# State space stage of a five-block network: where its normalisation, SiLU and first and last group stand in the order

## The chip, the cores and the metric

One core of a Trainium2 chip runs the whole program. The metric is the time of one execution on the device, in microseconds, of which the state space stage is one part in six. The engines are TensorE (matrix products; PE in the rows), VectorE (DVE), ScalarE (ACT), GpSimd (POOL) and SyncE (SP), which issues the loads. Each runs its own instructions in the order in which they are written, and the engines wait for each other by semaphores.

## The reference

`x` has shape (4, 1024, 256). The program computes six sublayers in turn, each on a layer norm of `x`: a gated recurrent layer, attention, the recurrent layer again, a mixture of experts, the state space layer (the "S" stage), the mixture again. The change touches the state space layer alone:

```
xn = rmsnorm(layernorm(x), norm_w)               # both norms in one scale and shift per token
z, x_ssm, B, C, dt_raw = split(xn @ in_proj_w.T) # 512, 512, 128, 128, 8 columns
x_conv = silu(conv_b + sum_k conv_w[k] * x_ssm shifted by k)       # 4 taps
dt = softplus(dt_raw + dt_bias);  dA = exp(-exp(A_log) * dt)       # 8 heads
h_t = h_(t-1) * dA_t + (dt_t * x_t) B_t;   y_t = h_t . C_t + D * x_t     # h_0 = 0
x = x + layernorm(x) + (y * silu(z)) @ out_proj_w.T
```

## The kernel before

The scan over 1024 positions is computed in chunks of 128. A tile is one chunk of one sequence. A group `p` (0 to 7, `PT` = 8) holds the four tiles (`b` = 0 to 3, `GT` = 4) of the four sequences at the same chunk, and the state `H` of each sequence goes from group to group. `n` = 4p + b is the tile's number. `groups` runs a loop over pairs of groups 0 to 5, and groups 6 and 7 behind it; its last argument `left` says whether two, one or no groups follow.

For a tile, `y` is a product within the chunk and one with the state: `tile_y` (L1509 by the decay matrix `dec`, L1512 by `H` and `rise`, the decays from the chunk's start times C). `tile_state` (L1520) computes what the chunk adds to the state. `tile_out` (L1528) multiplies the gated `y` by the output weights. The other engines feed it. ScalarE makes `dec` from `lb`, the loaded sums of decays (`decays`: eight L1630 and one L1633, for the tile `AHEAD` = 2 further on), reads the projections out of PSUM (`unit`: units dt, B, C, four of x, four of z, 11 a group, in three banks in turn), applies SiLU to the convolution (L1664) and to z, normalises a later group into `xn` (L1647) and turns `X` into its residual with `restore` (L1656). `hi` (L1639) and VectorE's `low` (L1724) split the turned `xn` for the products at full precision. VectorE also computes statistics (L1709 to L1717), convolution steps (L1735), `weigh` (L1765), `times_dt` (L1771), `gate` (L1781, L1786), `update_state` (L1792) and the residual (L1800). GpSimd makes scales and shifts in `norms` (L1853 to L1858), the rise products `scale_c` (L1867), `scale_x` (L1875) and `decay_state` (L1881). SyncE loads `lb` and `rise` for each tile, 512 KB each.

While group p is computed, the projections and the convolution of group p + 1 are made in pieces, one behind each tile (`piece`), and the normalisation of group p + 2 at `b` = `SCALE_AT`, its scales at `b` = `NORM_AT`. The order is written out by hand in each engine's `group`. At the border of two groups, these lines meet: TensorE's unit z3 reuses the bank of z0 and so waits for ScalarE's read of it; `turn_x` waits for SiLU of the whole convolution; VectorE has in its order `weigh` of the next tile 0, the statistics of group p + 2 and only then `times_dt` of tile 0, behind which the second `turn_x` and the first `tile_y` wait.

## Time and profile before

| | us |
|---|---|
| median of 3 runs | 1934.23 (1933.54 to 1936.37) |
| the profiled execution, its own time | 1933.88 |
| its span | 1932.1 |
| state space stage, 1322.9 to 1706.0 | 383.10 |
| in it TensorE busy | 339.28 |
| ScalarE busy | 273.38 |
| VectorE busy | 269.69 |
| GpSimd busy | 186.34 |

The time of an execution is a little more than its span, which runs from the first instruction to the last. Busy time of TensorE's matrix products, which overlap, is modelled; an engine's share says nothing by itself of what the others wait for. In the timeline rows the idle time before an instruction and what ended it stand in square brackets.

### The profile page before, as it was taken

How to read it: one execution, taken by the hardware profiler on the slowest of the kernel's cores; microseconds unless marked ns; L12 is line 12 of the kernel's file. 1: busy time of each engine (PE TensorE's matmuls, PEld its weight loads, DVE VectorE, ACT ScalarE, POOL GpSimd, SP SyncE). 2: the span in 40 equal slices, each digit the busy share in tenths (PEclk: the TensorE clock that was granted, in tenths of full speed). 3: DMA queues.
4: the chain of work that ended last, by engine and by line, in shares of the span. 5: the costliest groups of instructions: out<-in, count | busy, mean ns of one | idle time of the engine just before them, and what ended most of it. 6: DMA issues, size and time to landing. Idle time of an engine off the chain costs nothing. (4 is left out here: it accounts for less than half of the span.)

```text
span 1932.1 us, 30828 instructions
## 1 busy us (share of the span) xinstructions
PE 1752.0 (91%) x9742; PEld 1156.5 (60%) x9742; DVE 1340.6 (69%) x2878; ACT 1130.9 (59%) x1624; POOL 901.4 (47%) x654
## 2 busy tenths in 40 slices
PE   5999787999999999997999799997898899989998
PEld 4888673222222222227888677776676676767776
DVE  4545895777777777775555588885677777768886
ACT  3323588999999999994333222213777777622220
POOL 0001116999999999994002232211554445521111
PEclk9999898999999999998999999998999999999999
DMA  4000165534535435300000000001322222300000
GB/s 152 1 0 11 65 186 103 83 44 62 69 43 72 58 46 83 45 1 12 1 0 21 23 17 0 0 0 33 125 89 88 88 88 88 121 2 22 22 21 23
DMA packets 57640, 96.96 MB, mean 50 GB/s; under 512 B 7936, under 2 KB 29664, under 8 KB 57568
## 3 DMA queue, kind: packets, MB, share of 16 engines
q1 hardware_dynamic: 55392, 94.50, 21.7%
q10 hardware_dynamic: 2176, 1.55, 0.2%
q8 instruction: 39, 0.64, 0.1%
q14 instruction: 33, 0.27, 0.0%
HBM read 78.98 MB, written 17.04 MB: 50 GB/s over the span
## 5 line engine op out<-in xcount | busy, mean ns | idle before, releaser
L1232 POOL TENSOR_TENSOR att_weights<-att_weights 128x1024 f32<-128x1024 f32 x288 | 541.0, 1893 | 17.7 <-DVE att_weights L1176 7.3
L1176 DVE SCALAR_TENSOR_TENSOR att_weights<-att_weights,ps 128x512 f32<-128x512 f32 x576 | 370.1, 684 | 152.3 <-ACT att_weights L1152 150.5
L1152 ACT ACTIVATE att_weights<-att_weights 128x1024 f32<-128x1024 f32 x288 | 302.5, 1051 | 0.0
L1148 ACT ACTIVATE att_weights<-ps 128x1024 f32<-128x1024 f32 x288 | 294.1, 1022 | 9.9 <-PE ps L1094 5.6
L720 DVE SCALAR_TENSOR_TENSOR X<-ps,moe_gsel,X 128x256 f32 (+1 forms) x512 | 246.6, 484 | 64.4 <-PE ps L47 48.4
L1108 PE MATMUL ps<-att_weights,att_v_ones 128*32 128x512 f32 (+3 forms) x1536 | 288.8, 497 | 2.6 <-POOL att_weights L1232 2.5
L47 PE MATMUL ps<-w_experts_hi,moe_xh 128*128 128x512 f32 x512 | 205.2, 401 | 0.0
L47 PE MATMUL ps<-w_experts_hi,moe_xl 128*128 128x512 f32 x512 | 203.1, 397 | 0.0
L47 PE MATMUL ps<-w_experts_lo,moe_xh 128*128 128x512 f32 x512 | 201.6, 394 | 0.0
L313 ACT ACTIVATE ffn_gates<-ps,ffn_gate_bias 128x512 f32<-128x512 f32 x96 | 66.1, 688 | 207.2 <-PE ps L47 200.8
L1091 PE MATMUL ps<-q_stack,k_stack 128*128 128x512 bf16 (+3 forms) x384 | 116.8, 341 | 29.5 <-DVE att_weights L1176 19.8
L780 POOL TENSOR_TENSOR X<-X,moe_bias_sb 128x512 f32 (+1 forms) x32 | 41.5, 1298 | 207.6 <-DVE X L720 206.4
L103 POOL TENSOR_TENSOR ffn_rstd<-ffn_var,ffn_power 128x4 f32<-128x4 f32 x16 | 16.2, 1011 | 259.4 <-DVE ffn_var L135 259.4
L1091 PE MATMUL ps<-att_q_stack,att_k_stack 128*128 128x512 bf16 (+3 forms) x384 | 114.3, 332 | 22.6 <-DVE att_weights L1176 17.6
L1091 PEld LDWEIGHTS ps<-q_stack,k_stack 128*128 128x128 bf16 x384 | 37.3, 98 | 154.9 <-DVE att_weights L1176 143.0
L1091 PEld LDWEIGHTS ps<-att_q_stack,att_k_stack 128*128 128x128 bf16 x384 | 37.0, 96 | 149.7 <-DVE att_weights L1176 142.7
L47 PEld LDWEIGHTS ps<-w_experts_hi,moe_xh 128*128 128x128 f32 x512 | 96.0, 188 | 26.8 <-DVE X L720 3.3
L1108 PEld LDWEIGHTS ps<-att_weights,att_v_ones 128*32 128x32 f32 x1536 | 56.9, 108 | 90.0 <-issue 54.1
L47 PEld LDWEIGHTS ps<-w_experts_lo,moe_xh 128*128 128x128 f32 x512 | 96.1, 188 | 22.3
L47 PEld LDWEIGHTS ps<-w_experts_hi,moe_xl 128*128 128x128 f32 x512 | 96.1, 188 | 20.5
L629 ACT ACTIVATE moe_gT<-ps 96x512 fp32r<-96x512 f32 x16 | 9.5, 593 | 160.0 <-PE ps L560 160.0
L1867 POOL TENSOR_TENSOR ssm_rise<-ssm_rise,ssm_cT 128x512 f32<-128x512 f32 x64 | 94.5, 1502 | 18.0 <-DMA ssm_rise<-decays 18.0
(257 smaller groups left out, 3881.4 us busy)
## 6 DMA issues: line engine op xcount, KB each, us to landing
ssm_lb<-decays SPq DMA_DIRECT2D x32, 512.0 KB, 4.5
ssm_rise<-decays SPq DMA_DIRECT2D x32, 512.0 KB, 3.8
qk_parts<-qkv_part SPq DMA_DIRECT2D x32, 384.0 KB, 2.6
q_stack<-qk_parts SPq DMA_DIRECT2D x64, 128.0 KB, 4.5
k_stack<-qk_parts SPq DMA_DIRECT2D x64, 128.0 KB, 8.2
att_q_stack<-qk_parts SPq DMA_DIRECT2D x64, 128.0 KB, 4.6
att_k_stack<-qk_parts SPq DMA_DIRECT2D x64, 128.0 KB, 8.0
out<-X SPq DMA_DIRECT2D x8, 512.0 KB, 2.9
```

The source lines that it names most:

```text
L47: ins = pe.matmul(out, l(k), r(k), start=first and n == 0, stop=last and n == len(passes) - 1)
L103: pool.tensor_tensor(self.rstd[:, s], self.var[:, s], self.power[:, :], ALU.pow).then_inc(self.rstd_done, 1)
L313: act.activation(gates[:, m, gate], ring[:, u % RING], ACT.Tanh if gate == 2 else ACT.Sigmoid, bias=gate_bias[:, gate * KC + m:gate * KC + ...
L720: dve.scalar_tensor_tensor(out=x, in0=ring[:, e // 2, (e % 2) * C:(e % 2 + 1) * C], scalar=gsel[:, s, j, e:e + 1], in1=x, op0=ALU.mult, op ...
L780: pool.tensor_tensor(x, x, bias_sb[:, pair], ALU.add).then_inc(added, 1)
L1091: ins = pe.matmul(scores(u)[:, t, c:c + w], SK[s][:, h, kj * P:(kj + 1) * P], SQ[s][:, h, q:q + w], start=True, stop=not diagonal)
L1108: ins = pe.matmul(O(qb)[h * 2 * HD:(h + 1) * 2 * HD, q0:q0 + w], va[:, s, kj, h], Wt[:, u % WU, t, c:c + w], start=kj == 0, stop=m in BLOC ...
L1148: act.activation(Wt[:, u % WU], scores(u), ACT.Exp).then_inc(exp_done, 1)
L1152: act.activation(Wt[:, u % WU], Wt[:, u % WU], ACT.Ln, bias=1.0).then_inc(ln_done, 1)
L1176: dve.scalar_tensor_tensor(out=wt[:, t], in0=wt[:, t], scalar=LIMIT, in1=scores(u)[:, t], op0=ALU.min, op1=ALU.max).then_inc(max_done, 1)
L1232: pool.tensor_tensor(Wt[:, u % WU], Wt[:, u % WU], Wt[:, u % WU], ALU.mult).then_inc(sq_pool, 1)
L1867: ins = pool.tensor_tensor(heads, heads, cT[:, v, b].unsqueeze(1).broadcast_to([P, NH // 2, P]), ALU.mult)
```

## The change

In steady groups, `SCALE_AT` goes from 2 to 0 and the normalisation (now `apply`, then `restore`) stands behind that tile's decays, and the edges stand ahead of the decays at `b` = 2. SiLU of the convolution is two activations, the first of which waits for two convolutions of the four. `turn_in` waits for one unit fewer. Group 0 is taken out of the loop, and with it group 5: the loop now runs over pairs from 1 to 4. Group 0 has no state before it, so the products by `H`, `rise` and its loads, `scale_c` and `decay_state` are left out, and the update is a copy. Group 7 makes no state. In the head, `hi(0)` waits for its own load of `norm_w`, `restore(0)` follows it, the second statistics stand ahead of what waits for `neg_a`, `restore(1)` and the first two decays go into group 0 behind SiLU.

```diff
-        NORM_AT, SCALE_AT = 0, 2
+        NORM_AT, SCALE_AT = 0, 0
...
+            group(0, 0, 2)
+            with eng.Fori(0, PT // 2 - 2) as i:
                 group(i * 2 + 1, 1, 2)
+                group(i * 2 + 2, 0, 2)
+            group(PT - 3, 1, 2)
             group(PT - 2, 0, 1)
             group(PT - 1, 1, 0)
...
             def turn_in(p):
-                pe.wait_ge(unit_read, 3 + p * UNITS)
+                pe.wait_ge(unit_read, 2 + p * UNITS)
...
-                    for r in range(2):
+                    for r in range(0 if starts(p) else 2):
                         ins = pe.matmul(ps_y[r * DH:(r + 1) * DH, cols], H[:, b, 2 * f + r], rise[:, b % 2, 2 * f + r],
...
-                    tile_state(p, v, b)
+                    if left:
+                        tile_state(p, v, b)
...
-                act.wait_ge(conv_step, (p + 1) * FT * (TAPS - 1))
-                act.activation(xc[:, v], xc[:, v], ACT.Silu).then_inc(xc_done, 1)
+                half = FT // 2
+                for f in (0, half):
+                    act.wait_ge(conv_step, (p * FT + f + half) * (TAPS - 1))
+                    ins = act.activation(xc[:, v, f:f + half], xc[:, v, f:f + half], ACT.Silu)
+                ins.then_inc(xc_done, 1)
...
+                if starts(p):
+                    decays(0, v, 0, p)
+                    decays(1, v, 1, p)
...
+                    if starts(p) and b == 0:
+                        restore(p + 1)
...
+                    if left and b == 2:
+                        edges(p + 1, 1 - v)
                     if left or b + AHEAD < GT:
                         decays(n + AHEAD, v if b + AHEAD < GT else 1 - v, (b + AHEAD) % GT, p + (b + AHEAD) // GT)
...
-                        normalise(p + 2)
+                        apply(p + 2)
+                        restore(p + 2)
...
-            act.wait_ge(norm.xn_done, 1)
+            act.wait_ge(norm_in, 16)
+            hi(0)
...
-            dve.memset(H[:, :, :, :], 0.0).then_inc(h_done, GT)
...
+            statistics(1)
+            piece(0, 0, 0)
...
-                decay_state(v, p * GT, 0)
+                decays = left and not starts(p)
+                if decays:
+                    decay_state(v, p * GT, 0)
...
+            sp.dma_start(norm_w[:, :], c_dram["norm_w"]).then_inc(norm_in, 16)
```

How this moves instructions shows on two engines. ScalarE, in the loop at b = 0, before: from the decays of tile 2 to the read of unit B (`dtT` is the read of unit dt, `bT` of B).

```order
L1630 ACTIVATE ssm_dec<-ssm_lb,ssm_l_tok 128x128 x8
L1632 REGISTER_ALU
L1633 ACTIVATE ssm_dec<-ssm_dec 128x1024
L1567 ISA
L1582 ACTIVATE ssm_dtT<-ps,ssm_dt_bias 8x512
L1567 REGISTER_ALU
L1584 ACTIVATE ssm_bT<-ps 128x512
```

ScalarE in the changed kernel, from the end of the head through group 0 to the same place (`b_tm` is the last activation of the head, `zs` z, `xc` the convolution, `w_even_hi` the result of `hi`).

```order
L1622 ACTIVATE ssm_b_tm<-ps 128x512
L1592 ACT_TABLE_LOAD
L1592 ACTIVATE ssm_zs<-ps 128x512 x2
L1673 ACTIVATE ssm_xc<-ssm_xc 128x1024 x2
L1592 ACTIVATE ssm_zs<-ps 128x512 x2
L1677 ACT_TABLE_LOAD
L1638 ACTIVATE ssm_dec<-ssm_lb,ssm_l_tok 128x128 x8
L1641 ACTIVATE ssm_dec<-ssm_dec 128x1024
L1638 ACTIVATE ssm_dec<-ssm_lb,ssm_l_tok 128x128 x8
L1641 ACTIVATE ssm_dec<-ssm_dec 128x1024
L1647 ACTIVATE w_even_hi<-ps,ssm_norm_w 128x512 x2
L1663 ACTIVATE X<-X,ssm_shifts,ssm_grow 128x256 x4
```

```order
L1638 ACTIVATE ssm_dec<-ssm_lb,ssm_l_tok 128x128 x8
L1641 ACTIVATE ssm_dec<-ssm_dec 128x1024
L1590 ACTIVATE ssm_dtT<-ps,ssm_dt_bias 8x512
L1655 ACTIVATE ssm_xn<-X,ssm_shifts,ssm_scales 128x256 x4
L1663 ACTIVATE X<-X,ssm_shifts,ssm_grow 128x256 x4
L1592 ACTIVATE ssm_bT<-ps 128x512
```

The second piece follows the first directly. In it, `xn` and `X` now stand between `dtT` and `bT`, as they do in the loop. In the first, the two pairs of decays stand behind SiLU; before, they stood between `b_tm` and the table load:

```order
L1614 ACTIVATE ssm_b_tm<-ps 128x512
L1630 ACTIVATE ssm_dec<-ssm_lb,ssm_l_tok 128x128 x8
L1633 ACTIVATE ssm_dec<-ssm_dec 128x1024
L1630 ACTIVATE ssm_dec<-ssm_lb,ssm_l_tok 128x128 x8
L1633 ACTIVATE ssm_dec<-ssm_dec 128x1024
L1439 UNCONDITIONAL_BRANCH
L1439 ISA
L1567 ISA
L1584 ACT_TABLE_LOAD
```

So before, both first decays were done ahead of the loop; now they come after z and the convolution. The other engine is TensorE, at the end of the stage, before: the last products of tile 3 of group 7.

```order
L1509 MATMUL ps<-ssm_dec,ssm_xdt 64x128 x2
L1512 MATMUL ps<-ssm_rise,ssm_H 64x128 x2
L1528 MATMUL ps<-ssm_out_w,ssm_y 128x256 x4
L1520 MATMUL ps<-ssm_xd,ssm_b_tm 128x512
L1528 MATMUL ps<-ssm_out_w,ssm_y 128x256 x4
```

In the changed kernel L1520, the product for the state (its new line is not reached in this group), is gone from between the two `tile_out`, which follow each other.

## Rows read from the trace of the kernel before

**Rows 1.** the page, its first line

```profile
span 1932.1 us, 30828 instructions
```

**Rows 2.** busy time by stretch, group 1 (columns in the first line)

```profile
core 0: us, PE busy (x) PEld busy (x) DVE busy (x) ACT busy (x) POOL busy (x), PEclk, DMA share, GB/s
1412.00:1457.00 45.00, 40.42 (x281) 30.36 (x280) 33.41 (x64) 33.84 (x73) 23.58 (x21) 1.00 0.28 95
```

**Rows 3.** timeline, TensorE, the first tile_y of groups 1, 2, 6, 7 (start, us, engine, line)

```profile
1412.83 0.44 PE L1509 MATMUL ps<-ssm_dec,ssm_xdt 128*64 128x128 f32 x4
...
1458.03 0.44 PE L1509 MATMUL ps<-ssm_dec,ssm_xdt 128*64 128x128 f32 x4
...
1639.54 0.44 PE L1509 MATMUL ps<-ssm_dec,ssm_xdt 128*64 128x128 f32 x4
...
1681.37 0.44 PE L1509 MATMUL ps<-ssm_dec,ssm_xdt 128*64 128x128 f32 x4
```

**Rows 4.** timeline, TensorE, border of groups 1 and 2, with idle time before

```profile
1453.16 0.50 PE L47 MATMUL ps<-w_even_hi 128*128 128x512 f32 x1 [2.30 <-ACT ssm_zs L1584]
...
1455.63 0.63 PE L1497 MATMUL ps<-ident,ssm_xc 128*128 128x128 f32 x4 [0.81 <-ACT ssm_xc L1664]
```

**Rows 5.** timeline, ScalarE, the end of group 1

```profile
1438.90 0.81 ACT L1588 ACTIVATE ssm_xc<-ssm_xpad,ssm_conv_b,ssm_conv_w 128x512 f32<-128x512 f32 x1
...
1443.24 2.07 ACT L1647 ACTIVATE ssm_xn<-X,ssm_shifts,ssm_scales 128x256 f32 x4
1445.21 2.07 ACT L1656 ACTIVATE X<-X,ssm_shifts,ssm_grow  x4
...
1447.66 2.44 ACT L1630 ACTIVATE ssm_dec<-ssm_lb,ssm_l_tok 128x128 f32<-128x128 f32 x8
...
1451.21 1.28 ACT L1584 ACT_TABLE_LOAD   x1
...
1453.48 1.92 ACT L1664 ACTIVATE ssm_xc<-ssm_xc 128x2048 f32<-128x2048 f32 x1
```

**Rows 6.** timeline, ScalarE and GpSimd, b = 0 of group 1

```profile
1418.37 0.66 ACT L1582 ACTIVATE ssm_dtT<-ps,ssm_dt_bias 8x512 f32<-8x512 f32 x1
1424.72 0.60 ACT L1584 ACTIVATE ssm_bT<-ps 128x512 f32<-128x512 f32 x1 [5.68 <-PE ps L47]
1426.11 0.60 ACT L1584 ACTIVATE ssm_cT<-ps 128x512 f32<-128x512 f32 x1 [0.80 <-PE ps L47]
...
1420.31 0.22 POOL L1858 TENSOR_SCALAR ssm_grow<-ssm_scales 128x4 f32<-128x4 f32 x1
```

**Rows 7.** timeline, VectorE, group 1

```profile
1429.66 2.33 DVE L1735 SCALAR_TENSOR_TENSOR ssm_xc<-ssm_xpad,ssm_conv_w,ssm_xc 128x512 f32<-128x512 f32 x3
...
1444.42 6.28 DVE L1735 SCALAR_TENSOR_TENSOR ssm_xc<-ssm_xpad,ssm_conv_w,ssm_xc 128x512 f32<-128x512 f32 x6
...
1454.65 0.17 DVE L1717 TENSOR_SCALAR ssm_spread<-ssm_mv 128x4 f32<-128x4 f32 x1
1456.30 0.69 DVE L1771 TENSOR_TENSOR ssm_xdt<-ps,ssm_dt 128x512 f32<-128x512 f32 x1 [1.48 <-PE ps L1497]
```

**Rows 8.** timeline, VectorE and ScalarE, the head of the stage

```profile
1331.49 0.17 DVE L1837 TENSOR_SCALAR ssm_neg_a<-ssm_neg_a 128x8 f32<-128x8 f32 x1 [2.35 <-ACT ssm_neg_a L1691]
...
1336.37 2.08 ACT L1647 ACTIVATE ssm_xn<-X,ssm_shifts,ssm_scales 128x256 f32<-128x256 f32 x4 [3.88 <-POOL ssm_grow L1858]
...
1344.62 0.19 DVE L1745 SCALAR_TENSOR_TENSOR ssm_dt<-ssm_dta,ps 128x32 f32<-128x32 f32 x1 [9.47 <-ACT ssm_dta L1601]
```

**Rows 9.** timeline, VectorE, weigh of tile 3 in group 0

```profile
1389.43 1.27 DVE L1765 TENSOR_TENSOR ssm_dec<-ssm_dec,ssm_cb 128x1024 f32<-128x1024 f32 x1 [2.85 <-ACT ssm_dec L1633]
```

**Rows 10.** timeline, GpSimd and TensorE, the last group

```profile
1689.13 2.51 POOL L1867 TENSOR_TENSOR ssm_rise<-ssm_rise,ssm_cT 128x512 f32<-128x512 f32 x2
...
1697.38 0.44 PE L1509 MATMUL ps<-ssm_dec,ssm_xdt 128*64 128x128 f32 x4 [0.89 <-issue]
...
1703.40 1.96 PE L1528 MATMUL ps<-ssm_out_w,ssm_y 128*128 128x256 f32 x8 [1.27 <-DVE X L1800]
```

**Rows 11.** busy time by stretch (columns as in rows 2), start of group 0

```profile
1361.00:1367.00 6.00, 5.90 (x20) 4.80 (x21) 0.69 (x1) 4.82 (x7) 1.29 (x2) 0.50 0.00 0
```

More of the change, by code:

```diff
@@ L1435, in ssm_phase @@
         tile_of = lambda p, b: X[:, bass.ds(p * C + b * (PT * C), C)]
+        starts = lambda p: isinstance(p, int) and p == 0
         def groups(eng, group):
-            with eng.Fori(0, PT // 2 - 1) as i:
-                group(i * 2, 0, 2)
+            group(0, 0, 2)
+            with eng.Fori(0, PT // 2 - 2) as i:
                 group(i * 2 + 1, 1, 2)
+                group(i * 2 + 2, 0, 2)
+            group(PT - 3, 1, 2)
             group(PT - 2, 0, 1)
@@ L1502, in tile_y @@
                 pe.wait_ge(w_done, n + 1)
-                pe.wait_ge(cts_done, n + 1)
-                pe.wait_ge(h_done, n + 1)
+                if not starts(p):
+                    pe.wait_ge(cts_done, n - GT + 1)
+                    pe.wait_ge(h_done, n - GT + 1)
                 pe.wait_ge(y_done, FREE + n)
@@ L1518, in tile_state @@
                 pe.wait_ge(xd2_done, n + 1)
-                pe.wait_ge(h_done, GT + n)
+                if not starts(p) or b:
+                    pe.wait_ge(h_done, n)
                 pe.matmul(ps_h, b_tm[:, b], xd2[:, :, :].rearrange("p h d -> p (h d)"), start=True, stop=True)\
@@ L1649, in normalise @@
                 ins.then_inc(norm.xn_done, 1)
-                restore(p)
             def restore(p):
@@ L1687, in _ @@
             act.sem_inc(unit_read, 3)
-            act.wait_ge(norm.xn_done, 1)
+            act.wait_ge(norm_in, 16)
+            hi(0)
+            act.wait_ge(const_in, 16 * 7)
+            act.activation(neg_a[:, :], neg_a[:, :], ACT.Exp).then_inc(init_done, 1)
             restore(0)
-            act.wait_ge(const_in, 16 * 8)
-            act.activation(neg_a[:, :], neg_a[:, :], ACT.Exp).then_inc(init_done, 1)
-            hi(0)
-            normalise(1)
-            for b in range(GT):
-                piece(0, 0, b)
+            piece(0, 0, 0)
+            apply(1)
+            for b in range(1, GT):
                 if b == 2:
                     edges(0, 0)
-            decays(0, 0, 0, 0)
-            decays(1, 0, 1, 0)
+                piece(0, 0, b)
             groups(act, group)
@@ L1806, in group @@
                 times_dt(p, v, 1)
+                if starts(p):
+                    weigh(p, v, 0)
                 for b in range(GT):
@@ L1812, in group @@
                     gate(p, v, b)
-                    update_state(p, v, b)
+                    if left:
+                        update_state(p, v, b)
                     if b + AHEAD < GT:
@@ L1838, in _ @@
             dve.wait_ge(init_done, 4)
-            statistics(1)
-            for b in range(GT):
+            for b in range(1, GT):
                 piece(0, 0, b)
-            weigh(0, 0, 0)
             groups(dve, group)
@@ L1900, in group @@
                         norms(p + 2)
-                    if b + 1 < GT:
+                    if decays and b + 1 < GT:
                         decay_state(v, n + 1, b + 1)
-                    if left or b + AHEAD < GT:
+                    if left and (not starts(p) or b + AHEAD >= GT) or b + AHEAD < GT and not starts(p):
                         scale_c(p + (b + AHEAD) // GT, n + AHEAD, v if b + AHEAD < GT else 1 - v, (b + AHEAD) % GT)
-                if left:
+                if left == 2:
                     scale_x(p + 1, 1 - v, n + 1, 0)
@@ L1941, in spread @@
                     sp.dma_start(lb[:, b % 2], decay_dram[v, 0, rows].partition_broadcast(P)).then_inc(lb_in[b % 2], 16)
-                    if free:
+                    if not starts(p):
                         sp.wait_ge(y_summed, n - 1)
-                    sp.dma_start(rise[:, b % 2], decay_dram[v, 1, rows].partition_broadcast(P)).then_inc(rise_in[b % 2], 16)
+                        sp.dma_start(rise[:, b % 2], decay_dram[v, 1, rows].partition_broadcast(P)).then_inc(rise_in[b % 2], 16)
             spread(0, 0)
```

31 lines of the change are left out of this document (16 added, 15 removed).

## The prediction, on record before the changed kernel ran

> **What bounds the kernel now.** I read the page's span and the state space stage in a table of stretches first, then the stage's timeline, engine by engine. The profiled execution spans 1932.1 us [rows 1]. In one steady group of the stage TensorE is busy 40.42 of 45.00 us and no engine is full [rows 2], so the question is which wait ends last. A group is best timed by the first matmul of its first `tile_y`: 1412.83, 1458.03, 1639.54 and 1681.37 for groups 1, 2, 6 and 7 [rows 3]. That is 45.20 us from 1 to 2, 45.38 on average from 2 to 6, and 41.83 from 6 to 7.
>
> TensorE stands still at the border of two groups: 2.30 us until ScalarE has read the z units, 0.81 us until ScalarE has finished SiLU of the convolution [rows 4]. ScalarE has no idle entry in that stretch: it goes from the last tap at 1438.90 through decays, 2.07 us of `xn`, 2.07 us of restoring `X`, decays, the table load at 1451.21 and SiLU at 1453.48 [rows 5]. Earlier in the same group it waits 5.68 us for TensorE's unit B [rows 6]. So 4.1 us of normalisation sits on the chain that ends last while a gap lies open 20 us before. The reader should also look at VectorE, which is next: from the convolution at 1444.42 its timeline has no idle entry until the statistics end at 1454.82, and it waits only 1.48 us before `times_dt` at 1456.30 [rows 7].
>
> **The change, part by part.** *Normalisation at b = 0 (six groups).* GpSimd's last norm instruction ends at 1420.31 + 0.22 = 1420.5, ScalarE's `dtT` at 1419.0, and unit B is read at 1424.72 [rows 6]. 1420.5 + 2.07 + 2.07 = 1424.7: it fits, with nothing to spare, and the read of C behind it waits 0.80 [rows 6] and the one of x about as long, which could absorb 1.6. I cost it at 0 there. Behind it are queued the reads of B, C and x, for which TensorE waits, which matters for rival C. At b = 3 the chain loses 4.1 us. What is late next: ScalarE goes tap to 1439.7, edges 0.3, decays 3.5 (the step from 1447.66 to 1451.21 [rows 5]), to 1443.5; `b_tm` needs TensorE's transposes, which waited for the edges and start about 0.5 earlier, so it ends at 1444.2; decays to 1447.7; table load and two z reads 2.3 (1451.21 to 1453.48 [rows 5]) to 1450.05.
>
> *SiLU in halves.* The first half needs convolutions 0 and 1 only; each half is about 1.0 us (half of 1.92 [rows 5], taking the bounds 0.95 and 1.06, the latter by the 1024-column exponential). The second half needs the last convolution, at 1444.42 + 6.28 = 1450.70 [rows 7], before 1451.1. So `xc` is ready at 1452.1, not 1455.4. `turn_x` takes 0.7: 1452.8. But VectorE has its `weigh` and the statistics in front of `times_dt` and is free only at 1454.82 [rows 7]. From there 0.69 for `times_dt`, then the second `turn_x` and 0.53 to `tile_y`: 1456.1 against 1458.03. **A transition gains 1.9 us, not 4.1**, because VectorE takes over. There are five of these (0 to 1 up to 4 to 5): -9.5. Bounds 0 and -3.4 each.
>
> Group 6 has no statistics. VectorE is free at about 1452.8 in these coordinates, `xc` sets the pace, the turn of the next group ends at 1453.9 and `tile_y` comes at 1454.5: **-3.4** for 5 to 6. From 6 to 7 the normalisation was absent already, which is why that step takes 41.83; halving SiLU gives **-0.5**.
>
> A rule of the Trainium skill bears on this: "ScalarE: Activation LUTs", "What ACT_TABLE_LOAD costs", adds a drain of about 1.38 us to each load of 1.28. The trace has 1.28 at 1451.21 and the next activation follows within the 2.27 to 1453.48 that also holds two z reads [rows 5], so no drain is seen. By the rule `xc` would be ready 1.4 us later, still hidden behind the statistics five times and not at 5 to 6: the sum below would be 1.4 smaller.
>
> *The head.* VectorE waits 2.35 us for `neg_a`, behind ScalarE's restore, before it starts the second statistics [rows 8]. Now these run at once, and `hi(0)` waits for `norm_w` alone, so the low part ends at 1333.2 instead of 1335.1. `restore(0)` (2.1) moves behind `hi(0)` and ends at 1334.0, and `norms(1)` waits for it. Before, the second statistics ended 2.3 behind 1331.49, at 1333.8, and `xn` of group 1 followed 2.6 later at 1336.37 [rows 8]; now it comes 2.6 behind 1334.0, at 1336.5. But its restore (2.06) and `dtT` (0.66) no longer stand between it and unit B. B is read at 1338.5, C, x and the logarithm follow, and `dt` comes at 1341.5 instead of 1344.62 [rows 8]: -3.1. On SyncE `norm_w` moves ahead of four small loads of constants; the one large load stays last and was in before `neg_a` was touched, so it costs 0. The memset of `H` was hidden under GpSimd's norms: 0.
>
> *Group 0.* The convolution ends 3.1 earlier, near 1351. SiLU in halves 2.0, z 1.1 and table load 1.3 go ahead of the decays: 1355.3. Decays 0 and 1, 3.5 each, end at 1362.3; `hi(1)` 1.3, restore 2.1, decays 2 3.5, `dtT`, `xn`, restore 4.8: 1373.8. TensorE goes by `low(1)` (1365.1), unit dt 1.4, half a `tile_y` 0.9, out 2.0, state 1.0, transposes 0.6, and three units of 1.4: x is read near 1375.5. Before, `weigh` of tile 3 came at 1389.43 [rows 9], 7.3 us behind that read; now 1382.9. TensorE idles 4.6 to 5 us before `tile_y(0)` still. In the old group 0, after such an idle, it ran at a granted 0.50 of full clock, 1.2 GHz, for 6 us [rows 11]; I take 1.0 us off for it. **-5.5**, bounds -2 and -7. The 8 products by `H`, 8 of GpSimd's rise products and 4 loads of `rise` that group 0 leaves out (SyncE's queue holds its loads of `lb` alone) lie beside the ScalarE chain: 0 more.
>
> *Last group.* No state product (1.0), no decay on GpSimd (1.0), no update on VectorE (0.68). `tile_y(3)` was at 1697.38 because GpSimd's rise products for tile 2 started at 1689.13 behind a decay [rows 10]. Without it tile 2 waits for the gate of tile 1 (near 1690.1 instead of 1691.7), and tile 3 for the gate of tile 2, near 1695.5: -1.9. From there to the last `out`, 6.0 us were 1697.38 to 1703.40, with the update and the wait for its product before the residual [rows 10]; now 2.0 + 1.9 + 0.4 + 0.2 = 4.5: -1.5. Together **-3.4**.
>
> *Clock.* From group 2 to 6 the mean is 45.38, while group 1, with a granted clock of 1.00 [rows 2], took 45.20 [rows 3]: dips cost about 1 us in all. Shorter idles at the borders return half: -0.5.
>
> Sum: -9.5 - 3.4 - 0.5 - 5.5 - 3.4 - 0.5 = -22.8. The profiled execution took 1933.88, its span 1932.1 plus 1.8; the median of the runs is 1934.23, 0.35 more. 1933.9 - 22.8 = **1911**.
>
> **The rivals.** *A, VectorE gets faster too, and the transition gains 3.4.* Three convolution steps take 2.33 us when GpSimd is still, and six take 6.28 beside its rise products, against 4.66 at the former rate [rows 7]. If the new order pulled these apart, VectorE would be free 1.6 sooner and `xc` would bound: 5 x 1.3 more, 1904.5. Against it: both engines start by the same `tile_y`, so they still meet. The Trainium skill, "GPSIMD Engine Reference", "1. Specifications", says contention with VectorE arises for instructions with two SBUF inputs, which these are; the rows agree.
>
> *B, the clock.* The granted clock falls at every border and stays low through group 0's tiles, where TensorE now works in short bursts between ScalarE's decays. A dip costs up to 0.5 a group (0.18 is the mean of four groups, of which some have one [rows 3], and 1.0 us at half clock loses 0.5 [rows 11]), so 3 for six, and 3 in group 0, since 6 us at half clock took some 6 us for 20 matmuls [rows 11]: 1917. The Trainium skill, "TensorE: Matmul & The Clock Gate", "What's actually happening", says the throttled state is the default and that activity releases it; the row after the idle agrees.
>
> *C, the gap is too small; this is the side of no gain.* If GpSimd's norms come late by d, ScalarE holds up B, C and x; 1.6 us are absorbed, the rest enters the dt chain one to one. At d = 3.5 the six transitions gain nothing: 1911 + 13 = 1924. Past d = 5.4 (1.6 + 22.8/6) the kernel is slower than before, at d = 6 about 1938. For it: the sequence fits to the tenth. Against: norms wait for statistics that end before `tile_y`, and for the previous restore, which is now earlier too.
>
> *D, the change does not do what it says*: the activations that it splits and the code that it unrolls cost what it saves, 1932 to 1936. Nothing in the order speaks for it.
>
> **How the numbers follow.** Forecast (1906 to 1916) 0.66, A 0.08, B 0.15, C at no gain per group 0.05, C past its turning point 0.03, D 0.03. The range 1904.5 to 1920 takes in the forecast, A and B. What a measurement can tell from no change is 0.2%, about 4 us. Faster: 0.66 + 0.08 + 0.15 + 0.05 = 0.94 and a little of D; same 0.03; slower 0.03.
>
> **What would show it.** Right: `tile_y(0)` to `tile_y(0)` near 43.3 us in groups 1 to 5, 41.6 from 5 to 6; no 2.3 us wait on z; `xn` between `dtT` and `bT`, and `bT` within 0.2 of TensorE's end; `times_dt` directly behind the statistics; the first `dt` near 1341.5; 21 us from the last group's first `tile_y` to its end, against 24.4. Wrong: ScalarE's read of B waiting for nothing while TensorE waits for it (C), a clock of 0.5 in each border (B), `times_dt` waiting for its transposes (A).

## The result: 1.1% faster, 20.0 us of the 22.8 that the sum had

The changed kernel takes 1914.42 us (median of 4 runs, 1910.14 to 1915.94), the kernel before 1935.3 us beside it (4 runs). The ratio is 0.989, with a 95% interval of 0.9875 to 0.9904. The sum was made against the profiled execution, 1933.88 us; the profiled execution of the changed kernel took 1913.84 us, so 20.0 of the 22.8 us came. The page's first line, against [rows 1]:

```profile
span 1912.1 us, 30471 instructions
```

The stage is best read in a table of stretches from the first `tile_y` of a group to that of the next one. Here are groups 0 to 6 after the change (columns in the first line), to compare with [rows 2, 3]:

```profile
core 0: us, PE busy (x) PEld busy (x) DVE busy (x) ACT busy (x) POOL busy (x), PEclk, DMA share, GB/s
1359.65:1403.38 43.73, 38.27 (x217) 28.29 (x217) 32.80 (x63) 39.40 (x84) 11.48 (x12) 0.96 0.25 76
1403.38:1447.79 44.41, 41.75 (x281) 32.14 (x281) 33.62 (x64) 34.55 (x73) 23.26 (x22) 0.96 0.29 96
1447.79:1492.22 44.43, 41.59 (x282) 32.19 (x281) 33.64 (x64) 34.51 (x73) 23.34 (x22) 0.96 0.30 96
...
1581.08:1623.45 42.37, 41.61 (x281) 32.18 (x281) 31.65 (x54) 33.15 (x71) 23.41 (x22) 0.96 0.33 101
1623.45:1664.59 41.14, 39.17 (x274) 29.87 (x273) 31.43 (x54) 30.48 (x65) 19.73 (x17) 1.00 0.32 104
```

From group 1 to 5 a period lasts 44.4 us, where the prediction had 43.3 and the kernel before 45.2 to 45.7. TensorE's busy time is 41.59 to 41.75 us against 40.42 in [rows 2], for as many matmuls, and PEclk is 0.96. That is where the missing microseconds are: the matmuls themselves take longer. The border of groups 1 and 2 on TensorE, against [rows 4]:

```profile
1443.60 0.65 PE L1502 MATMUL ps<-ident,ssm_xc 128*128 128x128 f32 x4 [0.38 <-ACT ssm_xc L1673]
1444.27 1.06 PE L150 MATMUL ps<-ident,ssm_xn 128*128 128x128 f32 x8
1447.20 0.65 PE L1502 MATMUL ps<-ident,ssm_xc 128*128 128x128 f32 x4 [1.88 <-DVE ssm_xdt L1786]
1447.79 0.44 PE L1515 MATMUL ps<-ssm_dec,ssm_xdt 128*64 128x128 f32 x4
1448.06 0.56 PE L1518 MATMUL ps<-ssm_rise,ssm_H 128*64 128x128 f32 x4
1448.39 0.65 PE L1515 MATMUL ps<-ssm_dec,ssm_xdt 128*64 128x128 f32 x4
...
1451.11 1.33 PE L1527 MATMUL ps<-ssm_xd,ssm_b_tm 128*128 128x512 f32 x2
```

The wait for z is gone. TensorE waits 1.88 us for `times_dt` instead, and then a row of four products of `tile_y(0)` takes 0.65 us, against 0.39 at full clock (at 1454.69, in `tile_y(1)` of the same group): the granted clock is at half, 1.2 GHz. `tile_state` comes 3.32 us behind the first product; where the clock stays up it is 1.90. On VectorE `times_dt` stands directly behind the statistics, as predicted:

```profile
1446.40 0.16 DVE L1732 TENSOR_SCALAR ssm_spread<-ssm_mv 128x4 f32<-128x4 f32 x1
1446.47 0.68 DVE L1786 TENSOR_TENSOR ssm_xdt<-ps,ssm_dt 128x512 f32<-128x512 f32 x1
```

On ScalarE, at b = 0 of group 2, the normalisation stands in the gap of [rows 6]; the read of B follows with no idle entry, and the read of C waits 0.80 us as before:

```profile
1454.74 0.66 ACT L1590 ACTIVATE ssm_dtT<-ps,ssm_dt_bias 8x512 f32<-8x512 f32 x1
1456.86 2.08 ACT L1655 ACTIVATE ssm_xn<-X,ssm_shifts,ssm_scales 128x256 f32 x4 [1.46 <-POOL ssm_grow L1878]
1458.84 2.06 ACT L1663 ACTIVATE X<-X,ssm_shifts,ssm_grow  x4
1460.81 0.59 ACT L1592 ACTIVATE ssm_bT<-ps 128x512 f32<-128x512 f32 x1
1462.20 0.60 ACT L1592 ACTIVATE ssm_cT<-ps 128x512 f32<-128x512 f32 x1 [0.80 <-PE ps L47]
```

The head and group 0, against [rows 8, 9]: the first `dt`, TensorE's wait for the first decays, and `weigh` of tile 3.

```profile
1341.01 0.19 DVE L1760 SCALAR_TENSOR_TENSOR ssm_dt<-ssm_dta,ps 128x32 f32<-128x32 f32 x1 [7.98 <-ACT ssm_dta L1609]
...
1359.65 1.98 PE L1515 MATMUL ps<-ssm_dec,ssm_xdt 128*64 128x128 f32 x16 [4.92 <-DVE ssm_dec L1780]
...
1382.06 2.11 DVE L1780 TENSOR_TENSOR ssm_dec<-ssm_dec,ssm_cb 128x1024 f32<-128x1024 f32 x1 [2.78 <-ACT ssm_dec L1641]
```

And the last group, against [rows 3, 10]: its first `tile_y`, GpSimd's rise products for tile 2, the last `out` and the last residual.

```profile
1664.59 0.44 PE L1515 MATMUL ps<-ssm_dec,ssm_xdt 128*64 128x128 f32 x4
...
1670.66 3.18 POOL L1887 TENSOR_TENSOR ssm_rise<-ssm_rise,ssm_cT 128x512 f32<-128x512 f32 x2 [13.01 <-DMA ssm_rise<-decays]
...
1683.54 1.97 PE L1535 MATMUL ps<-ssm_out_w,ssm_y 128*128 128x256 f32 x8 [0.60 <-DVE X L1818]
1685.54 0.42 DVE L1818 TENSOR_TENSOR X<-X,ps 128x256 f32<-128x256 f32 x1 [2.15 <-PE ps L1535]
```

Term by term, in the two profiled executions:

| term | predicted | measured | from |
|---|---|---|---|
| head and group 0 | -5.5 | -7.4 | weigh of tile 3, 1389.43 to 1382.06 |
| border 0 to 1 | -1.9 | -2.1 | first tile_y of group 1, 1412.83 to 1403.38, less the above |
| groups 1 to 5, four periods | -7.6 | -4.0 | 181.66 to 177.70 |
| 5 to 6 | -3.4 | -2.7 | 45.05 to 42.37 |
| 6 to 7 | -0.5 | -0.7 | 41.83 to 41.14 |
| last group | -3.4 | -3.1 | 24.45 to 21.37 |
| clock | -0.5 | in the rows above | |
| sum | -22.8 | -20.0 | |

### The profile page after: what moved, and what is told of

It is laid out like the page before. It is cut to its first block and busy times, and to the rows that moved or that the text cites. A ratio compares the mean times of both kernels' runs of the same rounds, so it can differ in the third digit from the quotient of the medians.

```text
span 1912.1 us, 30471 instructions
## 1 busy us (share of the span) xinstructions
PE 1741.6 (91%) x9670; PEld 1152.8 (60%) x9670; DVE 1336.7 (70%) x2873; ACT 1132.6 (59%) x1632; POOL 876.1 (46%) x634
## 5 line engine op out<-in xcount | busy, mean ns | idle before, releaser
L1094 PE MATMUL ps<-ident,neg 128*128 128x128 bf16 x512 | 95.7, 222 | 0.0
```

The source lines that it names most:

```text
L1094: ins = pe.matmul(scores(u)[:, t, c:c + P], neg[:, :], ident16[:, :], start=False, stop=True)
```

## The experiments

Two theories stood against each other from the start. One: VectorE's statistics cap the border, TensorE's wait gathers in one piece of 1.88 us, the granted clock falls behind it, and `tile_y(0)` at half clock costs 1.1 us a group. The other: the half clock lies beside other work, and the gain is short for another reason (the halves of SiLU, contention, the gap). All kernels ran in 4 or 5 timed runs beside the kernel before. The times in the columns behind the ratio are of one profiled execution each. The stage's start is ScalarE's first table load in it (1323.10 in the changed kernel). The last column counts those of groups 1 to 5 where `tile_state` came 2.9 us or more behind the first product of `tile_y(0)`; where the clock stayed up it was 1.90. The column says nothing of falls elsewhere in a period: there are some, and the last section has them.

| kernel | us | ratio to before, 95% | first tile_y of group 1 after the stage's start | mean period, groups 1 to 5 | 5 to 6 | last group | `tile_y(0)` at half clock |
|---|---|---|---|---|---|---|---|
| before | 1934.6 to 1935.9 (medians of five sets) | | 89.6 | 45.4 | 45.05 | 24.45 | 0 of 5 |
| changed | 1914.42 | 0.9875 to 0.9904 | 80.3 | 44.4 | 42.37 | 21.37 | 5 of 5 |
| changed_again | 1915.92 | 0.9879 to 0.9912 | 80.5 | 44.4 | 42.38 | 21.49 | 5 of 5 |
| norm_move_alone | 1921.97 | 0.9919 to 0.9946 | 87.4 | 43.2 | 42.32 | 24.46 | 0 of 5 |
| norm_move_undone | 1923.62 | 0.9924 to 0.9952 | 82.5 | 45.5 | 44.69 | 21.73 | 0 of 5 |
| fill_border | 1909.22 | 0.9854 to 0.9885 | 80.7 | 43.3 | 41.13 | 20.74 | 0 of 5 |
| silu_whole | 1911.23 | 0.9864 to 0.9894 | 81.6 | 43.3 | 41.87 | 21.90 | 0 of 5 |
| stats_in_gap | 1899.18 | 0.9798 to 0.9825 | 80.7 | 41.3 | 41.13 | 21.92 | 0 of 5 |
| stats_gap_silu_whole | 1904.49 | 0.9831 to 0.9857 | 79.2 | 42.1 | 41.85 | 22.58 | 0 of 5 |
| stats_gap_restore_dve | 1899.03 | 0.9803 to 0.9829 | 78.4 | 41.3 | 41.14 | 21.63 | 0 of 5 |
| gap_more_work | 1914.40 | 0.9872 to 0.9902 | 81.7 | 44.4 | 42.36 | 21.26 | 4 of 5 |
| state_kept | 1919.39 | 0.9899 to 0.9926 | 81.4 | 44.4 | 42.36 | 24.39 | 5 of 5 |
| head_undone | 1918.59 | 0.9901 to 0.9928 | 86.8 | 43.3 | 41.12 | 21.19 | 0 of 5 |
| decays_ahead | 1916.97 | 0.9887 to 0.9917 | 84.6 | 44.5 | 42.38 | 21.27 | 5 of 5 |

### fill_border: work in TensorE's wait

```
         NORM_AT, SCALE_AT = 0, 0
+        FILL = 7
...
                     turn_in(p + 1)
+                if left == 2:
+                    for _ in range(FILL):
+                        pe.matmul(ps_y[:, 0:P], ident[:, :], ident[:, :], start=True, stop=True)
                 turn_x(p, v, 1)
```

> The changed kernel with 7 matmuls of the identity by itself (128x128, their result is overwritten) put on TensorE between the turn of the next group and the second turn_x, that is into the 1.88 us in which TensorE waits for VectorE; nothing else is changed and no wait is shortened. Theory (the half-clock stretch behind the border costs 1.14 us, the first tile_y ending at +3.3 us instead of +1.9): granted clock 1.00 behind the border, first tile_y in 1.9 us, period 43.3 instead of 44.4 in groups 1 to 5, 1914.4 - 5.7 = 1908.7 (1907 to 1911). Rival (the half clock lies beside VectorE's work, which sets the pace anyway, or the fill only moves the wait): no change, 1914 to 1916. If the clock falls in spite of the fill, idle time is not what brings it down.

It takes 1909.22 us, 5.2 less than the changed kernel. The same border on TensorE:

```profile
1445.48 1.73 PE L1547 MATMUL ps<-ident 128*128 128x128 f32 x14
1447.52 0.65 PE L1503 MATMUL ps<-ident,ssm_xc 128*128 128x128 f32 x4 [0.31 <-DVE ssm_xdt L1790]
1448.10 0.44 PE L1516 MATMUL ps<-ssm_dec,ssm_xdt 128*64 128x128 f32 x4
...
1450.00 1.12 PE L1528 MATMUL ps<-ssm_xd,ssm_b_tm 128*128 128x512 f32 x2
```

`tile_state` is back at 1.90 us behind the first product, and the table of stretches gives the predicted period with a full clock:

```profile
1404.80:1448.10 43.30, 41.82 (x295) 32.34 (x294) 33.37 (x64) 34.63 (x73) 23.74 (x22) 1.00 0.31 99
...
1578.02:1619.15 41.13, 40.10 (x282) 30.72 (x281) 31.43 (x54) 33.25 (x71) 23.54 (x22) 1.00 0.32 104
```

Seven useless matmuls (14 records) make the kernel faster; they fill idle time and change nothing else. The half clock cost 1.1 us a period (44.4 to 43.3), and 1.2 from 5 to 6 (42.37 to 41.13). The other theory falls. The interval of the ratio (0.9854 to 0.9885) overlaps a little with that of the changed kernel (0.9875 to 0.9904), but seven of the eight timed runs of the changed kernel, those of changed_again included, lie above all four of fill_border (1908.91 to 1911.31). The price of 1.1 us is also seen without any edit of the border: head_undone, below, has the same wait of 1.88 us and a full clock behind it, and its period is 43.3.

### norm_move_alone and norm_move_undone: the parts of the steady gain

The first is the kernel before with this edit; the second is the changed kernel with its reverse:

```
-        NORM_AT, SCALE_AT = 0, 2
+        NORM_AT, SCALE_AT = 0, 0
```

> The kernel before with one edit: the normalisation moved from b = 2 to b = 0; SiLU whole, head and groups 0 and 7 as before. Theory (VectorE's statistics cap the transition, and a half-clock stretch behind each border takes 1.1 us of the gain): the whole steady gain of the changed kernel comes from this edit, period 44.4 us from group to group instead of 45.4 (five times -1.0), and about -1.7 from group 5 to 6, where no statistics stand in front; sum -6.7, so 1927 to 1929. Rival 1 (the halves of SiLU carry part of the steady gain): periods 44.9 or more, 1930 to 1932. Rival 2 (no half-clock stretch when the halves are not there): periods 43.3, 1922.

> The changed kernel with the normalisation put back to b = 2, all else as changed. Theory: ScalarE is again what ends last at the border, halves of SiLU don't help since ScalarE itself is behind, so periods are again 45.2 to 45.7 us and the time 1914.4 + 7.7 = 1922 (1920 to 1924). Rival (the gain came from the halves): 1916 to 1918. The head, group 0 and the last group should keep their times of the changed kernel: first dt near 1341, 21.4 us from the last group's first tile_y to its end.

The move alone gives 1921.97 us, 13 less than before, with periods of 43.2 us. I had expected 44.4: my theory took the half-clock stretch for granted. Rival 2 had it right. The border on TensorE shows why there is none:

```profile
1450.67 0.63 PE L1497 MATMUL ps<-ident,ssm_xc 128*128 128x128 f32 x4 [0.64 <-ACT ssm_xc L1664]
1451.63 1.06 PE L150 MATMUL ps<-ident,ssm_xn 128*128 128x128 f32 x8 [0.34 <-ACT ssm_zs L1584]
1453.24 0.66 PE L1497 MATMUL ps<-ident,ssm_xc 128*128 128x128 f32 x4 [0.54 <-DVE ssm_xdt L1771]
```

TensorE waits 1.5 us in three pieces of 0.64, 0.34 and 0.54 us, where the changed kernel waits 2.3, of it 1.88 at once. The second kernel, at 1923.62 us, has the old periods again on average (45.5; 1922 expected), and its wait for z is 3.00 us, longer than the 2.30 of [rows 4]:

```profile
1447.53 0.80 PE L47 MATMUL ps<-w_even_hi 128*128 128x512 f32 x1 [3.00 <-ACT ssm_zs L1592]
```

The average hides the clock. The four periods are 46.61, 45.44, 45.13 and 44.80, with a granted clock of 0.93, 0.96, 0.96 and 1.00; at full clock the kernel before has 45.20. So with ScalarE late, the halves and the other edits of the steady groups bring 0.4 us a period at most, and the normalisation's move is worth 2.0 us at full clock (45.2 to 43.2), 2.2 on average. Group 0 was expected to keep the changed kernel's time and did not: at its end z is late too, and group 1's first `tile_y` comes 2.2 later.

### silu_whole: the halves cost time here

```
-                half = FT // 2
-                for f in (0, half):
-                    act.wait_ge(conv_step, (p * FT + f + half) * (TAPS - 1))
-                    ins = act.activation(xc[:, v, f:f + half], xc[:, v, f:f + half], ACT.Silu)
-                ins.then_inc(xc_done, 1)
+                act.wait_ge(conv_step, (p + 1) * FT * (TAPS - 1))
+                act.activation(xc[:, v], xc[:, v], ACT.Silu).then_inc(xc_done, 1)
```

> The changed kernel with SiLU of the convolution as one activation again, all else as changed. Theory (the halves bring the first turn_x forward while times_dt stays capped by VectorE's statistics, so TensorE's idle time gathers in one wait of 1.88 us, behind which the granted clock falls for 3.41 us and costs 1.14 a group): undoing them makes groups 1 to 4 faster, period 43.2 instead of 44.4 (4 x -1.2), no change from 5 to 6 (the half-clock stretch gone, 1.1, against SiLU 1.0 later), +0.7 from 6 to 7; sum -4.2, so 1910 (1908 to 1912). Rival (the stretch comes from the new order of edges and head, or of group 0): clock 0.96 and period 44.4 still, 1914 to 1916.

1911.23 us: without one part of the change the kernel is 3.2 us faster. Here too the intervals overlap (one run of four took 1914.12), and the periods of the trace, 43.3 against 44.4, carry the reading. The wait before the second `turn_x` shrinks as the first one grows, and the product for the state stands at 1493.21, 1.89 behind the first product:

```profile
1488.16 0.63 PE L1502 MATMUL ps<-ident,ssm_xc 128*128 128x128 f32 x4 [1.42 <-ACT ssm_xc L1671]
1490.73 0.66 PE L1502 MATMUL ps<-ident,ssm_xc 128*128 128x128 f32 x4 [1.02 <-DVE ssm_xdt L1783]
1491.32 0.44 PE L1515 MATMUL ps<-ssm_dec,ssm_xdt 128*64 128x128 f32 x4
...
1493.21 1.12 PE L1527 MATMUL ps<-ssm_xd,ssm_b_tm 128*128 128x512 f32 x2
```

Finishing `xc` a microsecond sooner can't move `times_dt`, which waits for VectorE; it only puts TensorE's wait into one piece. The halves do pay elsewhere in the same kernel: without them the first `tile_y` of group 1 comes 1.3 later, the step from 6 to 7 takes 41.88 instead of 41.14 and the last group 21.90 instead of 21.37.

### stats_in_gap: the cap removed, and stats_gap_silu_whole

```
-                if left == 2:
+                if starts(p):
                     statistics(p + 2)
...
                     if b:
                         residual(p, b - 1)
+                    if b == 1 and left == 2 and not (isinstance(p, int) and p == PT - 3):
+                        statistics(p + 3)
```

> The changed kernel with the statistics of group p+3 computed in group p at b = 1, where VectorE waits 4.7 us for ScalarE's logarithm, in place of those of group p+2 at the start of group p in front of times_dt. Theory: TensorE no longer waits 1.88 us for times_dt at the border; first tile_y of a group comes 1.8 us sooner, and without that idle time the granted clock stays at 1.00 behind the border, which gives 1.1 more: period 41.5 us instead of 44.4, 1914.4 - 9 - 5.7 = 1900 (1898 to 1903). Rival 1 (the clock falls anyway, whatever the idle time at the border): period 42.6, 1905. Rival 2 (ScalarE or TensorE take over at once, VectorE was not the cap): period 43.5 or more, 1911 to 1914.

> The kernel stats_in_gap (statistics of group p+3 at b = 1) with SiLU of the convolution as one activation. Theory: with VectorE's statistics gone from the border, the end of SiLU sets the pace there, so here the halves are worth what they were meant for: period 42.2 to 42.4 instead of 41.3 in groups 1 to 6, five or six times +0.9 and +0.7 from 6 to 7: 1899.2 + 5.5 = 1905 (1903 to 1907). Rival (the halves are worth nothing anywhere, or cost by their second fixed part): 1898 to 1901.

1899.18 us, 15 less than the changed kernel and 1.9% less than before. One border, and its period:

```profile
1487.19 0.63 PE L1502 MATMUL ps<-ident,ssm_xc 128*128 128x128 f32 x4 [0.78 <-ACT ssm_xc L1673]
...
1489.19:1530.44 41.25, 40.14 (x282) 30.73 (x281) 33.38 (x64) 34.54 (x74) 23.67 (x22) 1.00 0.32 102
```

The wait of 1.88 us is gone, the clock is full, and TensorE is busy 40.14 of 41.25 us. With SiLU whole on top of that it takes 1904.49 us, with periods of 42.04:

```profile
1486.03:1528.07 42.04, 40.04 (x281) 30.77 (x280) 33.48 (x64) 34.42 (x73) 23.76 (x22) 1.00 0.31 101
```

The halves are worth +0.8 us a period here and cost 1.1 in the changed kernel. Both kernels fell into their expected ranges, and their rivals fall. stats_in_gap, with stats_gap_restore_dve below, is also the fastest version of all.

### gap_more_work: how much room the gap has

```
                 ins.then_inc(norm.xn_done, 1)
+                if not isinstance(p, int) or p > 1:
+                    for b in range(GT):
+                        act.activation(extra[:, b * C:(b + 1) * C], tile_of(p, b), ACT.Identity,
+                                       bias=shifts[:, 0, b:b + 1], scale=grow[:, b:b + 1])
```

> The changed kernel with four more activations (2.06 us, the size of restoring X, written to a buffer of their own that nobody reads) between xn and restoring X at b = 0, in groups 0 to 5: it measures how much room is left in the gap that the normalisation went to. Theory (as predicted: 1.6 us are absorbed by the waits of the reads of C and x, the rest goes into the chain of dt one to one): +0.5 a group, 1914.4 + 2.5 to 3 = 1917 (1916 to 1919); the read of B 2.06 later, the logarithm 0.5 later. Rival (no room: ScalarE holds up TensorE's units at once): +2.06 a group, 1927. Rival (more room than I read): no change.

The median does not change: 1914.40 us. The groups of the profiled execution, which took 1916.19, do not all say the same. Group 3 kept a full clock and can be compared with a group of fill_border, 43.31 against 43.30 us; there 2.07 us more work cost nothing. Groups 1, 2 and 4, with `tile_y(0)` at half clock, took 45.03, 44.28 and 45.17 us instead of 44.4, 0.4 more on average, and group 0, where ScalarE is full, took 45.00 instead of 43.73. Group 3, group 4 and, on ScalarE, group 3 again:

```profile
1495.41:1538.72 43.31, 40.28 (x281) 30.77 (x280) 33.37 (x64) 36.22 (x77) 23.69 (x22) 1.00 0.28 98
1538.72:1583.89 45.17, 41.91 (x282) 32.34 (x281) 33.55 (x64) 36.11 (x77) 23.91 (x22) 0.96 0.30 94
```

```profile
1505.22 2.07 ACT L1661 ACTIVATE ssm_extra<-X,ssm_shifts,ssm_grow 128x256 f32 x4
1507.19 2.07 ACT L1668 ACTIVATE X<-X,ssm_shifts,ssm_grow  x4
1509.17 0.58 ACT L1593 ACTIVATE ssm_bT<-ps 128x512 f32<-128x512 f32 x1
1509.64 0.58 ACT L1593 ACTIVATE ssm_cT<-ps 128x512 f32<-128x512 f32 x1
1510.12 0.58 ACT L1593 ACTIVATE ssm_xpad<-ps 128x512 f32<-128x512 f32 x1
```

The three reads that came 1.39 us apart now follow each other at 0.48, so they catch up 0.9 us each over two steps. The room is about 2 us at full clock and some 0.4 less at half clock, where I had read 1.6. Added up, the extra work cost 2.5 us in this execution, near the theory's 2.5 to 3 though half of it lay in group 0, and the one border at which the clock did not fall gave 1.1 back. That the median shows nothing may be such borders in the other runs; they have no trace, so it is open.

### state_kept, head_undone, decays_ahead, stats_gap_restore_dve: head, group 0 and last group

state_kept gives both ends of the stage their state back. Its diff puts back the lines of the kernel before in `tile_y`, `tile_state`, `update_state`, `scale_c`, `decay_state`, the clearing of `H` and the loads of `rise`; in short:

```
-                    if left:
-                        tile_state(p, v, b)
+                    tile_state(p, v, b)
...
-                    if not starts(p):
+                    if free:
                         sp.wait_ge(y_summed, n - 1)
+                    if True:
                         sp.dma_start(rise[:, b % 2], decay_dram[v, 1, rows].partition_broadcast(P)).then_inc(rise_in[b % 2], 16)
```

> The changed kernel in which group 0 again has a state (H set to zero, the products by H, GpSimd's rise and decay products and the loads of rise) and the last group again makes one; head, order of group 0, normalisation and SiLU stay as changed. Theory: in group 0 that work lies beside ScalarE's chain of decays (0 to 1 us there, first tile_y of group 1 at most 1 us later), and only the last group pays: 24.4 instead of 21.4 us from its first tile_y to the end; 1914.4 + 3.1 + 0 to 1 = 1917.5 to 1918.5. Rival (the state products were part of what group 0 waited for, and explain that it gained 1.9 more than predicted): group 0 2 us longer or more, 1920 or more.

The last group takes 24.39 us again, 3.0 more, as expected. Group 0 takes 44.57 instead of 43.73 us, and the first `tile_y` of group 1 comes 1.1 later after the stage's start: near the expected 0 to 1, and not the 2 of the rival. The time, 1919.39, is 1 above the range; in the profiled execution the stage began 2.2 us later than in the changed kernel, in code that is the same. Over all the profiled executions the stage began between 1322.7 and 1325.8 us, so a time can differ by 3 us for reasons outside the stage, which no theory here explains.

```
-                    if starts(p) and b == 0:
-                        restore(p + 1)
...
+            act.wait_ge(norm.xn_done, 1)
+            restore(0)
             act.wait_ge(norm_in, 16)
-            hi(0)
             act.wait_ge(const_in, 16 * 7)
             act.activation(neg_a[:, :], neg_a[:, :], ACT.Exp).then_inc(init_done, 1)
-            restore(0)
-            piece(0, 0, 0)
+            hi(0)
             apply(1)
-            for b in range(1, GT):
+            restore(1)
+            for b in range(GT):
+                piece(0, 0, b)
                 if b == 2:
                     edges(0, 0)
-                piece(0, 0, b)
```

(VectorE's second statistics and first piece go behind `neg_a` again.)

> The changed kernel with the head of the kernel before (ScalarE restores group 0, then neg_a, hi, xn and the restoring of group 1; VectorE waits for neg_a before its second statistics), which also takes the restoring of group 1 out of group 0 again. Theory: the first dt comes 3.1 to 3.5 us later, but ScalarE, which sets the pace in group 0 (it waits for nothing from the first table load to the read of B), has 2.07 us less to do there; net +1.3, so 1915.7 (1915 to 1917). Rival (the head's gain arrives whole, the restoring in group 0 is hidden): +3.4, 1918.

My theory fell. The first `dt` came 3.5 later (21.39 after the stage's start against 17.91), but the first `tile_y` 5.4 later and that of group 1 6.5 later. Two steps were missing. The edges behind the second pair of units make TensorE wait for them before it turns B:

```profile
1344.97 0.19 DVE L1759 SCALAR_TENSOR_TENSOR ssm_dt<-ssm_dta,ps 128x32 f32<-128x32 f32 x1 [9.48 <-ACT ssm_dta L1609]
...
1351.14 0.66 PE L1489 MATMUL ps<-ident,ssm_bT 128*128 128x128 f32 x4 [1.74 <-ACT ssm_edge L1628]
...
1377.92 0.60 ACT L1592 ACTIVATE ssm_bT<-ps 128x512 f32<-128x512 f32 x1 [0.69 <-PE ps L47]
```

And in group 0 the 2.07 us of restoring that ScalarE no longer has turn into waits, here 0.69 for unit B: TensorE's chain is as long as ScalarE's, nothing is won back. The median is 1918.59, at the rival's 1918. The profiled execution, with a full clock behind all five borders, took 1914.95; the other four, with a mean clock of 0.978 or 0.979 instead of 0.981, took 1918.4 to 1918.8. These four have no trace, so how often the clock fell in them isn't known. In the trace the head's old order costs 6.5 us, more than either expectation had.

```
                 act.preload_act_table_set(LN_EXP_SET)
-                if starts(p):
-                    decays(0, v, 0, p)
-                    decays(1, v, 1, p)
...
+            decays(0, 0, 0, 0)
+            decays(1, 0, 1, 0)
             groups(act, group)
```

(VectorE's first `weigh` moves with them.)

> The changed kernel with decays 0 and 1 of group 0 in the head again, ahead of SiLU, as in the kernel before. Theory (part of group 0's gain comes from ScalarE working on decays while TensorE turns x, instead of TensorE waiting for SiLU behind them): first tile_y of group 0 about 4 us later, but then runs as in a steady group; ScalarE gets to decays 2 about 1.7 later, TensorE's chain makes it up to 3.6; +1.7 to +3.6 at weigh of tile 3 and in the total, 1916 to 1918. Rival (ScalarE does the same work in either order, nothing lost): 1914 to 1915, and the surplus of group 0 over the prediction comes from somewhere else.

The first `tile_y` of group 0 comes 4.2 us later after the stage's start, `weigh` of tile 3 2.7 later (61.7 against 59.0), as the theory had it. The median is 1916.97, +2.6, but only +1.1 against changed_again, so the trace carries this reading and not the time. From `weigh` of tile 3 to group 1's first `tile_y` another 1.6 us are lost (84.6 against 80.3), which the theory did not have.

stats_gap_restore_dve is stats_in_gap with the restoring of group 1 moved from ScalarE, in group 0, to four `tensor_scalar` on VectorE behind `times_dt(1)`.

> The kernel stats_in_gap, and in group 0 VectorE restores X of group 1 (four tensor_scalar behind the second times_dt, where it waits 2.91 us for the first decays) in place of ScalarE. Theory (ScalarE sets the pace in group 0): 2.07 us less there, 1899.2 - 2.1 = 1897 (1896 to 1898.5). Rival (TensorE's chain in group 0 is as long as ScalarE's, or VectorE's restoring delays the first weigh): 1899 to 1901.

The median is 1899.03 us, no change, at the rival's 1899 to 1901. The `dt` of group 1, computed in group 0, comes at 53.7 us after the stage's start in the one and 53.6 in the other. That agrees with head_undone: in group 0 ScalarE and TensorE are both full, and taking work from one alone wins nothing. The end of group 0 does differ between the two profiles, 80.7 against 78.4 for group 1's first `tile_y`, but the profiled execution of stats_in_gap was the slowest of its five (1903.81; the others 1898.15 to 1899.19), so that difference can't be put down to the edit.

### changed_again: does the clock fall in every execution?

> The changed kernel itself once more. The runs so far show that the wait of 1.88 us before the second turn_x does not bring the clock down in every execution: in head_undone, with the same wait at each border, the profiled execution had a granted clock of 1.00 behind all five borders and took 1914.95 us, the other four took 1918.4 to 1918.8. Theory (an execution either meets the half-clock stretch at its five borders or does not, worth 5 x 1.1 us less what the border gives back): times fall near 1910 or near 1914 to 1916, mean clock 0.981 with the former and 0.976 to 0.979 with the latter, and the profile shows which by its first tile_y, 1.9 or 3.3 us. Rival (the spread of the runs has nothing to do with the clock behind the borders): the profiled execution's time and its first tile_y do not go together.

All four timed runs took 1914.6 to 1917.3 us with a mean clock of 0.977 or 0.978, and the profiled one had half clock behind all five borders. Of the first set of the changed kernel, one run of four took 1910.14, with a mean clock of 0.981. That fits the theory, but the quick run has no trace, so that an execution of this kernel can go without the falls is not shown; and gap_more_work, with four of five, is neither of the theory's two kinds. The rival isn't refuted by one profile.

## Why the prediction was right, and where it was off

1911 was forecast and 1914.42 measured, inside the forecast's own range of 1906 to 1916, though it is B, in part, that happened. Some luck is in the number: the falls of the clock cost 5.6 us that the sum did not have, and the head and group 0 gave 1.9 more than it had. Without that surplus the time would have been 1916.3, just outside the range.

- *Normalisation at b = 0.* Right. It fits, the reads of C and x absorb it, and ScalarE's 4.1 us left the border. Rival C had no ground: `bT` starts within 0.1 of TensorE's end, and the room is about 2 us at full clock and 1.6 at half, where 1.6 was read.
- *"A transition gains 1.9 us, not 4.1, because VectorE takes over."* Right in mechanism and size: fill_border and norm_move_alone, where the clock stays up, have the period of 43.3 and 43.2 us that the text gives. stats_in_gap shows that VectorE was the cap: 2.0 us a period go when its statistics are moved (43.3 to 41.3).
- *The clock.* This term was wrong, and it is the step that failed: "Shorter idles at the borders return half: -0.5". I added up TensorE's idle time at the border and did not ask how it is split. It shrank from 3.5 us (2.30, 0.81, and 0.34 before the turn of `xn`) to 2.3, but 1.88 of it now lies in one wait just ahead of `tile_y(0)`, and five times the clock fell there. Rival B priced a fall at "up to 0.5 a group"; it measured 1.1. The rows behind that price were of falls that lay elsewhere: in the kernel before they hit the last unit of z and the turns ahead of `tile_y(0)`, and the two periods with such a fall were 45.74 and 45.54 us against 45.20, 0.3 to 0.5 more. `tile_y(0)` has next to none: its products took 3.3 instead of 1.9 us, and only 0.2 to 0.4 us of wait before `tile_y(1)` absorbed some. Five periods lost 5.6 us; B's other half, 3 us in group 0, did not come.
- *SiLU in halves.* I costed it as part of the 1.9 us. In the five capped borders it brought nothing for the end of SiLU and cost the 1.1 of the clock; in group 0 they saved 1.3 (silu_whole); from 5 to 6, where `xc` is the pace, they give 0.7 at full clock (41.87 in silu_whole, 41.13 in fill_border).
- *5 to 6: -3.4.* 42.37 with the half clock, 41.13 without: the step was undersized by 0.5 and lost 1.2 to the clock.
- *Head: -3.1 and group 0: -5.5 in all.* -3.6 and -7.4. The allowance of 1.0 for a slow clock was not needed: TensorE did run at half clock in the first `tile_y` of group 0 (0.50 from 1359.5 to 1362.5), but ScalarE set the pace around it. Edges ahead of the second pair of units, to which I gave 0.3, are worth up to 1.9 in the head (head_undone: 5.4 less the 3.5 of the first `dt`). ScalarE's table load stood at 1353.51, its decays ended at 1361.8 where I had 1362.3.
- *Group 0 without state: 0.* 0.8 to 1.1 (state_kept), small but not nothing. The text's 8 products by `H` are those of one tile; group 0 leaves out 32.
- *Last group: -3.4.* -3.1. GpSimd's rise products for tile 2 took 3.18 and waited for their load, where I had counted with the 2.51 of [rows 10].

## What to carry to other kernels

Idle time of an engine that sets the pace is not all alike: ask how long its longest single wait is and what stands right behind it, since TensorE's clock can fall there and a tight chain pays in full: 1.1 us a fall here, where falls beside looser work had cost 0.3 to 0.5. Speeding up one input of a join (here `xc`) when the other (VectorE's `times_dt`) is late only moves the wait; move the late one first, and then the early one is worth its price: the same halves of SiLU cost 1.1 us a group before and gain 0.8 after. Room in a gap is best measured by putting more work into it: here 2.07 us more cost nothing in a group at full clock, 0.4 on average in three at half clock and 1.3 in group 0, and the median showed none of it.
